# VectorE makes the low part of every fourth attention chunk, from masked values kept in PSUM

## The reference

```python
proj = x @ W
Wh, Ws = jnp.split(proj, 2, axis=-1)
scores = Wh @ Ws.T
a = jax.nn.softmax(scores, axis=-1) * adj
out = a @ Wh + x
return jax.nn.leaky_relu(out, 0.01)
```

## Time and profile before

| | us |
|---|---|
| median of 3 runs (lowest, highest) | 1616.38 (1614.1, 1616.49) |
| the profiled execution, its own time | 1616.64 |
| its span, first to last instruction | 1614.8 |
| mean granted TensorE clock | 0.995 of full |
| PE busy | 1555.8 |
| VectorE busy | 1152.6 |
| ScalarE busy | 1071.4 |
| POOL busy | 982.6 |

### The profile page before, as it was taken

How to read it: one execution, slowest core, us unless ns; L and a number is a source line. 1 busy time by engine, 2 the same in 40 slices (tenths; PEclk the granted TensorE clock), 3 DMA queues, 4 the chain that set the end, 5 groups by cost and what they waited for, 6 DMA issues and landing times.

```text
span 1614.8 us, 34761 instructions
## 1 busy us (share of the span) xinstructions
PE 1555.8 (96%) x12902; PEld 1540.1 (95%) x12902; DVE 1152.6 (71%) x2165; ACT 1071.4 (66%) x2090; POOL 982.6 (61%) x874
## 2 busy tenths in 40 slices
PE   5999999999999999999999999999999999999984
PEld 5999999999999999999999999999999999999984
DVE  7766766666665677777777777756777777777774
ACT  3579898988985566666666666646666666666663
POOL 2112222222220488888888888837888888888896
PEclk9999999999999999999999999999999999999998
DMA  4124444454441133333333335513333333333332
GB/s 147 40 53 118 118 119 117 119 149 114 117 105 33 40 98 100 99 98 99 99 99 99 100 101 178 173 46 86 99 99 99 102 103 99 104 101 99 99 109 68
DMA packets 88666, 163.36 MB, mean 101 GB/s; under 512 B 9265, under 2 KB 19376, under 8 KB 88240
## 3 DMA queue, kind: packets, MB, share of 16 engines
q1 hardware_dynamic: 60624, 113.41, 24.1%
q0 software_dynamic: 24336, 44.31, 11.2%
q10 hardware_dynamic: 3536, 3.41, 0.6%
HBM read 147.99 MB, written 13.11 MB: 100 GB/s over the span
## 4 chain that ended last, share of the span: by engine, by line
PE 80%; issue 6%; DVE 5%; POOL 5%; ACT 2%; DMA 0%; POOLq 0%; SPq 0%; DVEq 0%; ACTq 0%
PE PS L1133 29%; PE PS L1341 8%; PE PS L1344 8%; PE PS L1343 8%; PE PS L1208 5%; PE PS L1205 5%; PE PS L1207 5%; PE PS L1204 5%; PE PS L1206 5%; POOL FR L435 2%; POOL X L428 2%; DVE AF L957 1%; ACT FR L596 1%; DVE AF L930 1%; DVE PS L997 1%
## 5 line engine op out<-in xcount | busy, mean ns | idle before, releaser
L1133 PE MATMUL PS<-FR,RB 128*128 128x256 f32 x4056 | 536.6, 281 | 1.8 <-ACT X L578 1.8
L435 POOL TENSOR_TENSOR FR<-AF,FR 128x512 fp32r<-128x512 f32 x338 | 450.8, 1334 | 129.4 <-ACT FR L596 129.3
L1133 PEld LDWEIGHTS PS<-FR,RB 128*128 128x128 f32 x4056 | 500.9, 188 | 3.1 <-ACT X L578 3.0
L428 POOL TENSOR_TENSOR X<-X,ROW 128x512 f32<-128x512 f32 x294 | 384.8, 1309 | 82.3 <-ACT ROW L606 82.3
L1341 PE MATMUL PS<-FR,RA 128*128 128x256 f32 x1352 | 388.6, 287 | 18.8 <-POOL FR L435 18.2
L1344 PE MATMUL PS<-FR,RA 128*128 128x256 f32 x1352 | 379.7, 281 | 0.0
L1343 PE MATMUL PS<-FR,RA 128*128 128x256 f32 x1352 | 378.8, 280 | 0.0
L957 DVE TENSOR_TENSOR AF<-PS,AJ 128x512 f32<-128x512 f32 x338 | 231.7, 685 | 82.5 <-ACT PS L590 81.0
L1341 PEld LDWEIGHTS PS<-FR,RA 128*128 128x128 f32 x1352 | 254.4, 188 | 27.9 <-POOL FR L435 25.5
L401 POOL DMA_DIRECT2D STGT<-adjt x169 | 90.1, 534 | 296.1 <-PE PS L1208 296.1
L1343 PEld LDWEIGHTS PS<-FR,RA 128*128 128x128 f32 x1352 | 254.7, 188 | 0.0
(11 more groups left out here) (142 smaller groups left out, 2329.4 us busy)
## 6 DMA issues: line engine op xcount, KB each, us to landing
AJ<-adjt SPq DMA_DIRECT2D x338, 256.0 KB, 2.7
STGT<-adjt POOLq DMA_DIRECT2D x169, 256.0 KB, 3.0
xt_scratch<-ROW SPq DMA_DIRECT2D x12, 512.0 KB, 2.6
RB<-xt_scratch SPq DMA_DIRECT2D x12, 512.0 KB, 4.5
x_scratch<-X ACTq DMA_DIRECT2D x13, 256.0 KB, 2.2
ROW<-x_scratch SPq DMA_DIRECT2D x13, 256.0 KB, 3.1
out<-ROW SPq DMA_DIRECT2D x12, 256.0 KB, 3.3
X<-xt SPq DMA_DIRECT2D x1, 1536.0 KB, 11.3
```

The lines of the kernel that those rows point to most:

```text
L428: nc.gpsimd.tensor_tensor(slot, slot, MB.unsqueeze(1).broadcast_to([P, 2, 256]), ALU.subtract)\
L435: nc.gpsimd.tensor_tensor(LO[g % 2], WA[g % 2], HI[g % 3].bitcast(F32), ALU.subtract)\
L1133: last = nc.tensor.matmul(out, stationary(a, k), moving(b, k), start=(k == 0 and i == 0), stop=(k == K - 1 and i == 2))
```

## The change

Chunks with g % 4 == 3 (84 of 338) are marked as VectorE's. For such a chunk `total` goes ahead of `mask` on VectorE, `mask` writes its product over the exponentials in their PSUM bank and not into WA, `high` reads that bank, and the low part is made by VectorE from that bank in the step in which PE weighs the chunk, after `maximum` and `weighted` of that step and ahead of `total` and `mask` of the next chunk. POOL leaves these chunks out. The exponentials of chunk g+2, which go to the same bank, wait for VectorE's low part of g. The other chunks are as before; the counts of POOL's semaphore take account of those left out.

```diff
+def by_vector(g):
+    return g % 4 == 3
+
+def pool_lows(g):
+    return sum(not by_vector(i) for i in range(g + 1))
+
+def vector_lows(g):
+    return sum(by_vector(i) for i in range(g + 1))
...
@@ gpsimd, the loop over steps
-                if x is not None:
+                if x is not None and not by_vector(x):
                     low(x)
@@ scalar, exponent(g)
                 if g >= 2:
                     act.wait_ge(sum_d, g - 1)
+                if g >= 2 and by_vector(g - 2):
+                    act.wait_ge(vlo_d, vector_lows(g - 2))
@@ scalar, high(g)
-                nc.scalar.activation(HI[g % 3], WA[g % 2], ACT.Copy).then_inc(hi_d, 1)
+                nc.scalar.activation(HI[g % 3], PS[:, 2 + g % 2, :] if by_vector(g) else WA[g % 2], ACT.Copy)\
+                  .then_inc(hi_d, 1)
@@ vector, mask(g), vector_low(g) and total(g)
                 dve.wait_ge(exp_d, g + 1)
                 dve.wait_ge(adj_full[g % NADJ], 16 * (g // NADJ + 1))
+                if by_vector(g):
+                    dve.wait_ge(sum_d, g + 1)
+                    to = PS[:, 2 + g % 2, :]
+                else:
+                    if g >= 2:
+                        dve.wait_ge(alo_d, pool_lows(g - 2))
+                    to = WA[g % 2]
+                nc.vector.tensor_tensor(to, PS[:, 2 + g % 2, :], ADJ[g % NADJ], ALU.mult).then_inc(mask_d, 1)
+
+            def vector_low(g):
+                dve.wait_ge(hi_d, g + 1)
                 if g >= 2:
-                    dve.wait_ge(alo_d, g - 1)
-                nc.vector.tensor_tensor(WA[g % 2], PS[:, 2 + g % 2, :], ADJ[g % NADJ], ALU.mult).then_inc(mask_d, 1)
+                    dve.wait_ge(av_mm, g - 1)
+                nc.vector.tensor_tensor(LO[g % 2], PS[:, 2 + g % 2, :], HI[g % 3].bitcast(F32), ALU.subtract)\
+                  .then_inc(vlo_d, 1)
 
             def total(g):
+                if by_vector(g):
+                    dve.wait_ge(exp_d, g + 1)
@@ vector, the loop over steps
                     weighted(A_END[v - 1])
+                a = A_AT.get(v)
+                if a is not None and by_vector(a):
+                    vector_low(a)
+                if x is not None and by_vector(x):
+                    total(x)
                 if x is not None:
                     mask(x)
                 if A_END.get(v - 1) is not None and v - 1 != LAST1:
                     residual(A_END[v - 1], 0)
-                if x is not None:
+                if x is not None and not by_vector(x):
                     total(x)
@@ tensor, weigh(g)
-                pe.wait_ge(alo_d, g + 1)
+                if by_vector(g):
+                    pe.wait_ge(vlo_d, vector_lows(g))
+                else:
+                    pe.wait_ge(alo_d, pool_lows(g))
```

More of the change, by code:

```diff
@@ L254, in two_graph_blocks @@
         alo_d = sem("alo_d")
+        vlo_d = sem("vlo_d")
         av_mm = sem("av_mm")
```

## The result

The change made the kernel slower by 1.9%: 1645.61 us median (1644.67 to 1646.32) against 1616.43, a ratio of 1.0186 with a 95% interval of 1.0174 to 1.0198. The forecast was 1628.3 with a range of 1616 to 1640. The sign held. The forecast size, 12 us, was less than half of the measured 29, and the mechanism held only in part: three causes of cost were priced at nothing.

The account below looks back on a forecast made before the run. PE was taken to bound layer 2, VectorE's queue to delay layer 1, POOL to pace only the tail. Block ends 11.7, weight split 0.6, seam 0.9, tail -1.2 gave +12.0 us: 1628.3 against 1616.38, range 1616 to 1640.

Parts of the forecast that it names:

- What bounds it: Long stretches: PE bounds layer 2, VectorE's queue makes layer 1's low parts late; POOL sets the pace only at the end.
- (a): Layer 1, seam and last chunks: PE waits for POOL, those waits go, VectorE's low part stays hidden; 1604.8 us, chance 0.13.
- (b): Layer 1's present waits soak up the moved slots and the last chunks gain 5 us: +1.5, 1618 us, chance 0.12.
- (c): Inside blocks too, the held PSUM bank makes exp(g+2) late: 18 us more, 1646 us, chance 0.05.
- The added instruction: VectorE's 84 new low parts: 0.6 us each charged to its queue, 0.69 to whoever waits for the result.
- b = 2 mod 4: Ends of blocks numbered so: low part of chunk g_e+1 (g_e the block's last) follows the weighting, PE starts 0.6 us later.
- b = 0: Ends of blocks numbered 0 mod 4, chunk third after the block's last: 0.8 us stays in layer 1, nothing in layer 2.
- b = 3: Ends of blocks numbered 3 mod 4: the slot delays the row sum, an estimated 0.25 us left in both layers.
- First: Layer 1 from 600 to 1060 us, layer 2 from 1100 to 1540: removing POOL's 84 low parts was worth nothing.
- The tail: Last chunks, four of them VectorE's: 0.3 us gained per period of four chunks; -1.2 us, between 0 and -5.
- The block with the one-off split: Weight split holding VectorE from 978.89 to 980.6 us: chunk 139's low part late, +0.6 us above a slot.
- The seam: Chunk 167's low part stands behind a low part of Wh: +1.1 us, of which about 0.9 is kept.

Follow-up runs that it names:

- the inner chunks: Against the changed kernel, VectorE keeps only its 45 chunks at places 4 to 11, none at weight split, seam or tail: 1615.65 us, ratio 1.0003 to the kernel before.
- the 39 chunks alone: Against the changed kernel, VectorE keeps only its chunks at places 12 and 0 to 3, weight split, seam and tail: 1646.22 us, ratio 1.0186 to the kernel before.

## Why the prediction was right in sign and wrong in size

**What bounds it** held. POOL's freed 108 us were worth nothing in the long stretches, the inner chunks cost nothing (ratio 1.0003), and the new waits of PE are those on VectorE, none inside a block but at the weight split and in the tail. Rivals (a), relief of POOL, and (b), absorption by layer 1's waits, fell with the first result; (c), the held bank, fell with the inner chunks.

**The added instruction** was priced rightly at 0.6 us of queue and 0.68 of result, and for b = 2 mod 4, where little else acts, the ends came out near what was worked (0.64 for 0.6 in layer 1, 0.80 for 0.6 in layer 2). The Trainium skill's sentence that I weighed (VectorE: DVE Perf Modes, "The DRAIN you can't avoid") would have changed little; independent instructions went on starting 0.6 us apart, and the same paragraph goes on to say that a next op that is not held starts earlier, with which the trace agrees. The slot's sum was low: the block ends had 13.2 us for 11.7, since layer 1's b = 0 and the b = 3 ends were dearer and layer 2's b = 0 ends cost 0.5 where I had nothing, and no tail gain came with it: 15.2 by itself where I had 12 with everything.

**The steps that failed** are three terms put at nothing. By intervals the change cost 30.5 us for a forecast of 12.0; the slot explains 3.2 of the 18.5 between them, and these three, with what the parts do to each other, the rest.

**First**, "in the two long stretches that is time nobody waits for, so it is worth nothing there". It was worth less than nothing: POOL's next instruction came sooner and held up VectorE's, 6.4 us at eleven block ends, and the run that took the collisions away is 6 us faster. I named the work that hid the edit but not what the freed engine would do with the time. The Trainium skill (Advanced Engine Details and Errata, "Mode Summary") notes that VectorE's second SBUF port is shared with GpSimd and that GpSimd's instructions and VectorE's 2-port ones block each other. The runs show such blocking for plain fp32 instructions with two SBUF inputs, of which that note doesn't speak.

**Second**, "The edits of the mask ..., of the high part ... and of the total (now ahead of the mask) add no instruction", with zero taken. The durations were as said (in place in PSUM 0.70 us, the high part from PSUM 0.60). But the swap brought a wait of VectorE on its own last instruction, and in the replay of the block ends I moved mask by no more than the slots. The diff had that wait in plain sight. In the changed kernel 4.4 us are left for the order and all else, of which some 2.4 are read from the ends with b = 1 and 2 (six at 0.36, five at 0.05). Tried alone it cost 17 us, some 11 by the wait, but the test's conditions are not the change's. The Trainium skill says in the section named above (VectorE: DVE Perf Modes, "The DRAIN you can't avoid"), of eight copies with and without a semaphore between them, that "the semaphore costs nothing extra here"; here it cost 0.2 to 0.3 us each time (0.81 for 0.60, and 0.88 in the test), on a queue with no slack.

**Third**, and not in the text at all: a wait can cost more than its length. Three stretches at half clock took 1.5 us each, about 4.5 together.

**The tail** gave 0.2 us where I had 1.2: a period of four chunks took 9.9 us for 9.96, where I had 0.3 less. That mask's wait for total, 0.2 us more in the loop that I had made 2.5, is the cause is my reading; no run shows it. The block with the one-off split had 0.8 for 0.6 and 0.6. The seam was 2.5 for 0.9, 1.5 of it the clock: with the same chunk 167 on VectorE and no half-speed stretch, the interval there has 1.0 in the run with the 39 chunks alone.

Not settled: the split of the 30.5 us (slot 15.2, collisions 6.4, clock 4.5, the order and all else 4.4) takes the slot's cost in the kernel before to be its cost in the changed one, which no run shows; collisions and clock were measured in the changed kernel itself. Nor is it shown why the clock falls behind one wait and not behind another of the same length.

## What to carry to other kernels

When work moves from a fast-enough engine to another, replay the receiving engine's queue at its fullest place with every semaphore in the diff, those on its own earlier instructions above all, and then ask what the relieved engine will start sooner and whom it meets there. Move work where the giving engine is the pace (here ten chunks in the tail, 4 us gained) and not in a fixed ratio over the whole kernel. An order that needs no new wait is worth looking for first: in the tail, with another PSUM bank as the target, none was needed.

## What the runs showed of the hardware

- A VectorE instruction with both inputs in SBUF that was issued while a POOL elementwise instruction ran ended a fixed time after that one: leaky 0.55 to 0.56 us in five of five (1.39 us for 0.69), fold_sum 0.28 in six of six (0.94 to 0.97 for 0.43, 0.60 once), and the low part from SBUF 0.55 in all 26 long ones (up to 1.84 for 0.68). In the other order POOL's is the longer one (1.60 for 1.29 us). With one input in PSUM none of the 24 low parts that began during a POOL instruction was longer.
- A VectorE instruction that waits for the end of the one before starts 0.72 to 0.88 us after it (mask behind total 0.81 in the changed kernel, 0.88 in the test of the order), one that doesn't 0.6, for 128 x 512 fp32 elements.
- After PE waits of 2.1 to 2.5 us the granted clock fell to half for 3.4 us in two blocks and at the seam of the changed kernel, and not in a third block with a wait of the same length. In other runs it fell after 1.77 us once in three, and did not after 2.12 at the seam. Each fall cost about 1.5 us (block 4's 3.26 against block 8's 1.73; the seam's 2.5 with, 1.0 without).
